# A decoder layer on one core: the QKV projection of three token tiles in three f32r passes, with the front's banks and the loads rearranged

## The reference

```python
x = x + attn(layernorm(x), Wq, Wk, Wv, Wo)        # 32 query heads, 8 key/value heads of 16
x = x + xattn(layernorm(x), ctx, Wq2, bq, Wk2, bk)  # context 2 x 512 x 512
x = x + ffn(layernorm(x), w_gate, w_up, w_down)     # ternary weights, inner size 1376

def attn(x, Wq, Wk, Wv, Wo):
    q, k, v = x @ Wq, x @ Wk, x @ Wv                # 512, 128 and 128 columns
    q, k = rope(q), rope(k)
    scores = q @ k.T / 4, causal mask, softmax      # per head
    return (attn @ v) @ Wo
```

## Time and profile before

| what | value |
|---|---|
| device time, median of 3 runs | 246.92 us (246.51 to 247.06) |
| the profiled execution's own time | 245.21 us |
| its span in the profile | 243.5 us |
| PE busy | 230.0 us, 94% |
| DVE busy | 153.6 us, 63% |
| ACT busy | 119.5 us, 49% |
| POOL busy | 36.1 us, 15% |

### The profile page before, as it was taken

How to read it: one execution, slowest core, us unless ns; L and a number is a source line. 1 busy time by engine, 2 the same in 40 slices (tenths; PEclk the granted TensorE clock), 3 DMA queues, 4 the chain that set the end, 5 groups by cost and what they waited for, 6 DMA issues and landing times.

```text
span 243.5 us, 4183 instructions
## 1 busy us (share of the span) xinstructions
PE 230.0 (94%) x1454; PEld 160.6 (66%) x1454; DVE 153.6 (63%) x561; ACT 119.5 (49%) x199; POOL 36.1 (15%) x61
## 2 busy tenths in 40 slices
PE   8799999999998979999999998899999999999994
PEld 3367657677766757655776454688888777767771
DVE  2689389996775687687571358986645655343323
ACT  2036576666849636662597370843643223323230
POOL 3330000372222224221220221000000010000000
PEclk9999999999999997999999999999999999999999
DMA  5999200001650460346000054000000000020002
GB/s 155 393 401 405 87 0 1 1 3 48 241 182 1 119 232 0 91 133 245 3 2 2 0 191 156 1 3 0 0 1 3 0 0 3 0 89 0 0 3 86
DMA packets 8981, 19.97 MB, mean 82 GB/s; under 512 B 1056, under 2 KB 1440, under 8 KB 8960
## 3 DMA queue, kind: packets, MB, share of 16 engines
q1 hardware_dynamic: 8384, 19.60, 22.7%
q10 hardware_dynamic: 576, 0.10, 0.2%
HBM read 18.58 MB, written 1.05 MB: 81 GB/s over the span
## 4 chain that ended last, share of the span: by engine, by line
PE 81%; DVE 7%; DMA 5%; issue 2%; ACT 2%; POOL 1%; DVEq 0%; SPq 0%; ACTq 0%; POOLq 0%
PE ps L1193 16%; PE ps L1208 8%; PE ps L1032 7%; PE ps L1058 7%; PE ps L1131 6%; PE ps L1084 6%; PE ps L1019 4%; PE ps L1040 4%; PE ps L1286 3%; PE ps L1300 3%; PE ps L1146 3%; PE ps L1115 3%; PE ps L1257 3%; DMA raw<-up_dram 2%; PE ps L1250 2%
## 5 line engine op out<-in xcount | busy, mean ns | idle before, releaser
L912 DVE CUSTOM_DVE_ANT_0 ps<-ps,maskf 128x128 f32<-128x128 f32 (+1 forms) x128 | 41.1, 397 | 3.0 <-PE ps L1250 3.0
L492 POOL TENSOR_SCALAR_AFFINE_SELECT prob<-prob 128x512 f32<-128x512 f32 x32 | 20.1, 651 | 94.1 <-ACT prob L688 94.1
L688 ACT ACTIVATE prob<-ps 128x1536 f32<-128x1536 f32 x16 | 23.2, 1451 | 16.4 <-PE ps L1289 16.4
L1032 PE MATMUL ps<-wqkv,xnT 128*128 128x512 f32 (+1 forms) x64 | 22.3, 493 | 0.7 <-ACT xnT L509 0.7
L576 ACT CAST in_hi<-inter 128x256 f16<-128x256 f32 (+1 forms) x22 | 8.9, 406 | 24.0 <-DVE inter L874 24.0
L1193 PE MATMUL ps<-h_hi,gate_q 128*128 128x256 f16 (+1 forms) x88 | 20.4, 273 | 0.0
L1193 PE MATMUL ps<-h_lo,up_q 128*128 128x256 f16 (+1 forms) x88 | 20.4, 273 | 0.0
L1193 PE MATMUL ps<-h_lo,gate_q 128*128 128x256 f16 (+1 forms) x88 | 20.4, 273 | 0.0
L1193 PE MATMUL ps<-h_hi,up_q 128*128 128x256 f16 (+1 forms) x88 | 20.4, 272 | 0.0
L874 DVE TENSOR_TENSOR inter<-gate_s,ps 128x256 f32<-128x256 f32 (+1 forms) x22 | 9.2, 420 | 16.4 <-PE ps L1193 15.4
L912 DVE DVE_READ_ACCUMULATOR2_ANT mx<- 128x1 f32 x128 | 18.5, 145 | 0.0
(11 more groups left out here) (161 smaller groups left out, 468.4 us busy)
## 6 DMA issues: line engine op xcount, KB each, us to landing
raw<-gate_dram SPq DMA_DIRECT2D x1, 2752.0 KB, 17.2
raw<-up_dram SPq DMA_DIRECT2D x4, 688.0 KB, 4.9
ctxT<-ctxT_dram SPq DMA_DIRECT2D x2, 1024.0 KB, 5.9
ctx_n<-ctx_dram SPq DMA_DIRECT2D x2, 1024.0 KB, 8.7
wqkv<-wqkv_dram SPq DMA_DIRECT2D x4, 384.0 KB, 6.3
raw<-down_dram SPq DMA_DIRECT2D x2, 768.0 KB, 4.6
x<-x_dram SPq DMA_DIRECT2D x4, 256.0 KB, 5.8
xwq<-xwq_dram SPq DMA_DIRECT2D x1, 1024.0 KB, 9.1
```

Source lines behind the costliest of these rows:

```text
L492: nc.gpsimd.affine_select(out=v, in_=v, compare_op=ALU.is_ge, fill=0.0, base=0, pattern=[[0, GROUP], [1, P]], channel_multiplier=-1).then_ ...
L688: nc.scalar.activation(prob[:, i % 2, :], ps[:, 3:6, :].rearrange("p a b -> p (a b)"), ACT.Exp, scale=DH ** -0.5).then_inc(exp_done, 1)
L912: nc.vector.tensor_tensor_reduce(scores, scores, mask, 1.0, LOWEST, ALU.add, ALU.max, to).then_inc(max_done, 1)
L1032: mm = nc.tensor.matmul(out, xnT[:, k, t * P:(t + 1) * P], wqkv[:, k, lo:hi], start=(k == 0), stop=(k == KD - 1))
```

## The change

The projections of tiles 1, 2 and 3 are computed as three products of f32r operands in place of one of f32. Tile 0 stays as it was. For this the weights are split once, in four chunks of 128 x 640: ACT rounds each to f32r (`w_hi`), POOL subtracts to get the rest (`w_lo`). The transposed tile is split too: ACT's copy out of PSUM now rounds (`xnT_r`), and DVE subtracts that from the bank (`tile_low`, `xnT_lo`). DVE no longer copies two of the ten early stacks, ACT copies them all. The projections and stacks use other banks. Side pieces stand in other slots, and the loads of the up weights, of the context of batch 0 and of the down weights are spread over more steps; every up chunk has a semaphore of its own.

```diff
-        TILE_BANK = (0, 5, 6, 7)
+        TILE_BANK = (0, 5, 6, 0)
+        ST_BANKS = (5, 1, 6, 2)
...
-            ([], [("abs", 0, 1), ("abs", 0, 2)], [("pq", 3)]),
-            ([("abs", 0, 3)], [("rot", 3, 0)], [("pk", 3), ("st", 10), ("hi", 3, 0)]),
-            ([("hi", 3, 1), ("rot", 3, 1)], [("a", 0, 0), ("part", 0)], [("st", 11)]),
+            ([("abs", 0, 1)], [("abs", 0, 2)], [("pq", 3)]),
+            ([], [("rot", 3, 0), ("abs", 0, 3), ("pk", 3)], [("rot", 3, 1), ("part", 0), ("a", 0, 0)]),
+            ([], [("lo", 3, 0), ("st", 10), ("hi", 3, 0)], [("st", 11), ("hi", 3, 1)]),
...
-            ([("abs", 1, 0)], [], [("abs", 1, 1), ("a", 2, 0)]),
-            ([], [], [("abs", 1, 2), ("u", 0)]),
-            ([("abs", 1, 3)], [("part", 1)], [("u", 1)]),
+            ([], [("abs", 1, 0)], [("abs", 1, 1), ("a", 2, 0)]),
+            ([], [("abs", 1, 2)], [("u", 0)]),
+            ([], [("part", 1), ("abs", 1, 3)], [("u", 1)]),
...
-        UP_LOADS, CTX_LOAD, DOWN_LOADS = {4: (0, 1), 5: (2, 3)}, 8, {11: (0, 1), 12: (2, 3)}
+        UP_LOADS, CTX_LOAD, DOWN_LOADS = {4: (0,), 5: (1,), 6: (2,), 7: (3,)}, 8, {11: (0,), 12: (1,), 13: (2, 3)}
...
-                    load_context(0)
+                if CTX_LOAD <= i < CTX_LOAD + KD:
+                    k = i - CTX_LOAD
+                    sp.dma_start(ctxT[0][:, k, :], ctxT_d[0, k * P:(k + 1) * P, :]).then_inc(ctxT_in[0], 16)
+                if CTX_LOAD + KD <= i < CTX_LOAD + KD + PT:
+                    k = i - CTX_LOAD - KD
+                    sp.dma_start(ctx_n[0][:, k, :], ctx_d[0, k * P:(k + 1) * P, :]).then_inc(ctx_in[0], 16)
...
-            for n in range(1, TT):
-                root(n)
+            def w_low(k):
+                pool.wait_ge(w_high, k + 1)
+                nc.gpsimd.tensor_tensor(w_lo[:, k, :], wqkv[:, k, :], w_hi[:, k, :].bitcast(F32), ALU.subtract
+                                        ).then_inc(w_low_done, 1)
+
+            root(1)
+            w_low(0)
+            root(2)
+            w_low(1)
+            root(3)
+            w_low(2)
+            w_low(3)
...
             tile_T(0)
+            for k in range(KD):
+                act.wait_ge(wqkv_in[k], 16)
+                nc.scalar.copy(w_hi[:, k, :], wqkv[:, k, :]).then_inc(w_high, 1)
             tile_T(1)
             heads_high(0, 0)
             heads_high(0, 1)
             tile_T(2)
             tile_T(3)
-            stacks(0, 1)
+            stacks(0, 5)
             heads_high(1, 0)
             heads_high(1, 1)
-            stacks(1, 2 * NST)
+            stacks(5, 2 * NST)
...
+            def tile_low(t):
+                dve.wait_ge(xnT_sb, t + 1)
+                nc.vector.tensor_tensor(xnT_lo[:, :, (t - 1) * P:t * P],
+                                        bank(TILE_BANK[t]).rearrange("p (k q) -> p k q", k=KD),
+                                        xnT_r[:, :, t * P:(t + 1) * P].bitcast(F32), ALU.subtract
+                                        ).then_inc(xnT_low, 1)
...
                 stats(t)
+                if t == 3:
+                    tile_low(1)
                 normalise(t, lambda: t >= 2 and dve.wait_ge(xnT_ps, t - 1))
...
                 rotate(t, 1)
                 if t == 1:
-                    stacks()
+                    tile_low(3)
                 heads_low(t, 0)
                 heads_low(t, 1)
+                if t == 0:
+                    tile_low(2)
...
+            def project_high(out, t, e):
+                pe.wait_ge(xnT_sb, t + 1)
+                pe.wait_ge(w_high, KD)
+                pe.wait_ge(xnT_low, t)
+                for k in range(KD):
+                    nc.tensor.matmul(out, xnT_r[:, k, t * P:(t + 1) * P], w_hi[:, k, HEAD_COLS[e]],
+                                     start=(k == 0), stop=False)
+                    nc.tensor.matmul(out, xnT_lo[:, k, (t - 1) * P:t * P], w_hi[:, k, HEAD_COLS[e]],
+                                     start=False, stop=False)
+            def project_low(out, t, e):
+                for k in range(KD):
+                    pe.wait_ge(w_low_done, k + 1)
+                    mm = nc.tensor.matmul(out, xnT_r[:, k, t * P:(t + 1) * P], w_lo[:, k, HEAD_COLS[e]],
+                                          start=False, stop=(k == KD - 1))
...
             tile_T(0)
+            pe.wait_ge(xnT_sb, 1)
+            project_first(qkv_bank(0, 0), 0).then_inc(qkv_ps, 1)
+            tile_T(1)
+            project_first(qkv_bank(0, 1)[:, 0:QKV - D], 1).then_inc(qkv_ps, 1)
+            project_high(qkv_bank(1, 0), 1, 0)
+            tile_T(2)
+            project_high(qkv_bank(1, 1)[:, 0:QKV - D], 1, 1)
+            project_low(qkv_bank(1, 0), 1, 0).then_inc(qkv_ps, 1)
+            project_low(qkv_bank(1, 1)[:, 0:QKV - D], 1, 1).then_inc(qkv_ps, 1)
             tile_T(3)
             stacks(0)
+            project(qkv_bank(2, 0), 2, 0).then_inc(qkv_ps, 1)
+            stacks(1)
             pe.wait_ge(rope_read, 4)
             pe.wait_ge(v_sb, 2)
-            pe.wait_ge(xnT_sb, 3)
-            project(qkv_bank(2)[:, 0:D], 2, 0).then_inc(qkv_ps, 1)
-            stacks(1)
-            project(qkv_bank(2)[:, D:QKV], 2, 1).then_inc(qkv_ps, 1)
+            project(qkv_bank(2, 1)[:, 0:QKV - D], 2, 1).then_inc(qkv_ps, 1)
```

More of the change, by code:

```diff
@@ L68, in decoder_layer @@
         gate_q = sb("gate_q", [P, KD, INNER], BF16)
+        front = ExitStack()
+        sb("front_places", [P, QK], F32, front)
+        xnT_lo = sb("xnT_lo", [P, KD, 3 * P], F32R, front)
+        front.close()
         up_q = sb("up_q", [P, KD, INNER], BF16)
@@ L125, in decoder_layer @@
         ksT = sb("ksT", [P, KV // 2, B * T], F32R, early)
+        front = ExitStack()
+        w_lo = sb("w_lo", [P, KD, QKV], F32R, front)
+        front.close()
         prob = sb("prob", [P, 2, 6 * T], F32, early)
         early.close()
+        w_hi = qsT[1][:, :, :].rearrange("p a b -> p (a b)")[:, 4 * T:4 * T + KD * QKV].rearrange("p (k n) -> p k n", k=KD)
         late = ExitStack()
@@ L162, in decoder_layer @@
         m_placed = [sem("m_placed0"), sem("m_placed1")]
+        up_in = [sem(f"up_in{k}") for k in range(KD)]
         out_stored = sem("out_stored")
@@ new lines, in decoder_layer @@
+            ([("whole", 1, 3), ("tern", 1, 1), ("tern", 1, 2)], [("tern", 1, 3), ("wo", 1)], [("n2", 0), ("n2", 1),
+             ("a", 3, 0), ("xT", 1, 0)]),
+            ([], [("xT", 1, 1)], [("a", 3, 1), ("high", "wo", 0), ("low", "wo", 0)]),
+            ([("abs", 2, 0), ("abs", 2, 1), ("g", 0, 0), ("abs", 2, 2)], [("high", "wo", 1), ("abs", 2, 3)],
+             [("low", "wo", 1), ("g", 0, 1), ("high", "wo", 2)]),
+            ([("low", "wo", 2), ("xs", 0), ("part", 2)], [("abs", 2, 4)], [("xs", 1), ("xpT", 0), ("high", "wo", 3)]),
@@ L508, in tile_T @@
                 act.wait_ge(xnT_ps, t + 1)
-                nc.scalar.copy(xnT[:, :, t * P:(t + 1) * P],
+                nc.scalar.copy((xnT if t == 0 else xnT_r)[:, :, t * P:(t + 1) * P],
                                bank(TILE_BANK[t]).rearrange("p (k q) -> p k q", k=KD)).then_inc(xnT_sb, 1)
@@ L531, in stacks @@
                 for s in range(lo, hi):
[L532 to L535 removed]
+                    act.wait_ge(stT_ps, s + 1)
+                    nc.scalar.copy(st_target(s), bank(st_bank(s)).rearrange("p (a q) -> p a q", a=4)
+                                   ).then_inc(stT_act, 1)
             def sum_abs(w, c):
                 rows, at, n = chunks(w)[c]
[L540 to L543 removed]
+                if w == 1:
+                    act.wait_ge(up_in[c], 16)
+                elif c == 0:
+                    act.wait_ge(raw_in, 16 * (1 if w == 0 else 2 + KD))
+                if w == 1 and c == 0:
+                    act.wait_ge(rope_read, 2 * TT)
                 nc.scalar.activation(tern_target(w)[0:rows, at:at + n], raw[0:rows, at:at + n], ACT.Abs,
@@ L1317, in _ @@
             pe.wait_ge(consts_set, 3)
-            for s in range(2 * NST - 3, 2 * NST):
+            for s in range(2 * NST - len(ST_BANKS), 2 * NST):
                 st_evacuated(pe, s)
```

119 lines of the change are left out of this document (52 added, 67 removed), and 7 rows, old and new, of the table BESIDE.

## The result

The changed kernel takes 249.41 us, the median of 4 runs (249.25 to 249.57); the kernel before takes 246.71 in 4 runs (244.84 to 247.06). The ratio is 1.0116, 95% interval 1.0068 to 1.0165: about 1.2% slower, where 243.1, faster, was forecast. The profiled execution took 249.52 us with a span of 247.8, against 245.21 and 243.5 before: 4.3 us to explain.

The account below looks back on a forecast made before the run. PE's work plus its few holes bounds the kernel, DVE nearly full at 36.4 to 49.5 us. Front +0.1, tile 3 +0.2, up -1.35, context -2.8: -3.85 from 246.92 gives 243.1 us, range 240.8 to 246.2.

Parts of the forecast that it names:

- the one on the down loads: Later steps: the last down chunks leave one step later, close to the sums that read them; no cost counted.
- new holes between 100 and 156 us, where I count none: Sign that the prediction is wrong: PE gets new idle times in that stretch, where it expected none.
- The front: Up to group 0: POOL's 1.4 us subtractions hold three DVE normalisations; PE waits 1.75 against 1.66 gained, 0.1 us lost.
- The prediction's own rate: Front's end: with normalisations held three times, each 0.1 us more of POOL's subtraction costs 0.3 us.
- held twice: Rival, front: last normalisation waits for POOL's third and fourth subtractions; 244.5 us, or 246.0 with a clock fall; chance 0.2.
- no hold: Rival, front: POOL's subtraction leaves DVE alone, or takes 0.75 us; PE saves 1.66 without waits; 241.3 us, chance 0.19.
- Tile 3: Early steps where DVE is full: PE's 0.83 us saving costed at nothing; 0.2 lost, between 1.0 lost and 0.5 gained.
- The load terms: Steps 8 and 11: spread up loads gain 1.35 us; spread context loads, with the clock there, gain 2.8.
- The f32r prices: Projection products on PE: f32r passes at 0.23 us a step for 512 columns and 0.13 for 256.
- The rows from step 7 on: Later steps, with AFTER's reordering: no change of time counted; AFTER changes no amount of work, PE is full there.

Follow-up runs that it names:

- e1: after with the last three down chunks issued at i = 12, in place of one at 12 and two at 13; 244.20 us, ratio 0.9883 to the kernel before.
- e4: The kernel before with only the down loads moved as in the change, one step later; 247.01 us, ratio 1.0013 to the kernel before.
- e5: after with late down loads kept and, in step 15, gT's evacuation ahead of the second sum in ACT's order; 247.30 us, ratio 1.0009 to the kernel before.
- e7: e1 with POOL waiting for the normalisations of tiles 1, 2 and 3 before its first three subtractions; 241.94 us, ratio 0.982 to the kernel before.
- after: The changed kernel, with the whole change, against the kernel before; 249.41 us, ratio 1.0116.
- e11: e8 with the three POOL waits of e7; 240.34 us, ratio 0.9782 to the kernel before.
- e8: after's front, f32r products and separate semaphores, with BESIDE, AFTER, UP_LOADS and DOWN_LOADS of the kernel before; 242.37 us, ratio 0.9857 to the kernel before.
- e10: e9 with the three POOL waits of e7; 238.94 us, ratio 0.9719 to the kernel before.
- e3: The kernel before with only the context spread over eight DMAs and a semaphore for each up chunk; 240.35 us, ratio 0.9772 to the kernel before.
- e12: e3 with after's table rows from step 7 on and its AFTER; 239.65 us, ratio 0.9768 to the kernel before.
- e9: e1 with the kernel before's table rows for steps 0 to 6; 239.81 us, ratio 0.977 to the kernel before.

## Why the prediction was wrong

**The step that failed** is the one on the down loads: "the last down chunks leave one step later than before, close to the sums that read them", costed at nothing. Measured: +5.9 us in the profile, 5.2 by e1's median. The lateness was seen and its price was not worked out. What was to be added: the load leaves at 117.66 behind a context chunk and needs 7.6 us to the sum that reads it, the new row of step 15 puts two sums of 1.25 us ahead of `gT`, and PE waits for `gT`: 3.06 us, and 2.82 more by the clock behind it. e4 shows that the late load alone is free, e5 that the second sum, with the fall of the clock, is 3.3 us of it in the profile and 2.1 in the median. The warning "new holes between 100 and 156 us, where I count none" is what happened.

**The front**: the mechanism was right, the size off. The prediction had POOL start just before the normalisation and hold it for the whole subtraction, three times; all three rows show it, and e7 shows the cost. But it took 1.4 us for the subtraction, for 640 columns; it is 1.82 for 768. Normalisations of 1.6 were forecast and 2.03 found; the rotation of tile 0, forecast for 17.5, began at 19.12, and the front's last projection at 32.8 in place of 30.7. The prediction's own rate, 0.3 us for each 0.1 of the subtraction, gives 0.1 + 3 x 0.42 = 1.4 us; e1, whose front has no fall of the clock, lost just that (27.57 against 26.14 before). After's other 0.8 of the +2.2 are the late start of tile 1's normalisation, 0.4, which is none of the change's doing as far as the rows show, and 0.4 that wasn't counted: half the clock from about 18 to 22 us, behind PE's hole of 2.30 (the rival "held twice" had such a fall in it). e5, which has the same fall, has the same front, 27.97 us. The figure of the Trainium skill (GPSIMD Engine Reference, 3.1 Elementwise — side-by-side cycle accounting), scaled to 768 columns, is an estimate of 1.7 us, near the 1.82 measured. The rival "no hold" had it that PE then saves its 1.66 us and waits for nothing. With POOL's waits nothing is held, and 0.3 to 0.5 us arrive: PE waits for `w_lo` instead, 1.24 us in e7 and 0.58 in e11, a wait that neither the forecast nor a rival has.

**Tile 3**: "0.2 lost, between a loss of 1.0 and a gain of 0.5". The product did get shorter, and PE only waited longer for the maxima (0.81 to 0.83 us in e1, e7 and e8, in place of 0.18), as argued. e8 puts the f32r part at nothing: 14.82 us for groups 0 to 3, before 14.87. The new rows cost some 1.2 us without the clock and 2.5 to 3.0 with it, by e7 and e10, outside the bounds. The clock was missed: the argument counted PE's holes there by their length only.

**The load terms** were right: -1.7 and -3.1 in the profile against -1.35 and -2.8. There is no hole for `oT` in step 8 or for the placed maxima in step 11, and the clock is 1.00 from 88 to 98 us. The nearness has some luck in it: the forecast was made from one profiled execution, and e3 makes them 6.5 us in the median, since falls of the clock behind these two holes go too, and the profiled execution had one of them only.

**The f32r prices** were right: 0.23 us a pass of 512 columns and 0.12 of 256 (0.13 forecast). **The rows from step 7 on** and `AFTER`, costed at nothing, gain 0.5 to 0.7 us (e12). Of the rivals, "held twice" had the front's fall of the clock, but not its mechanism: the last normalisation ended at 19.20, with POOL's third subtraction, and not at 20.9 with the fourth. None had the down load.

From after's 249.41 the way down is: 5.2 for the down load (e1), 2.3 for the three holds (e7), 3.0 for the rows of steps 0 to 6 (e10); by the ratios, which allow for the chips, 5.7, 1.6 and 2.5. What is left, 8 us below before, is for the most part spread loads (6.5, e3) and later rows (0.7, e12); the f32r passes have half a us of it at most.

What stays open: why the clock falls at 45 to 50 us in some executions of a kernel and not in others, why after's down load took 1.3 us longer than e4's, and why e9's first subtraction came late.

## What to carry to other kernels

A load that is moved "close to its reader" is to be costed as a chain: when it leaves its queue and behind what, how long it takes, what the reading engine has queued between the landing and the next thing that PE needs. Work given to POOL isn't free because POOL is idle: a subtraction that starts first holds a tensor-scalar or a two-input add of DVE to its end, and a wait that lets DVE's short instruction go first cost POOL 0.66 us each time, and three of them gave 2.3 in the median. The bill comes later: the last subtraction ends later, and PE waits for it. Shorter products pay only where PE's own work sets the end: with the operand split on slower engines, tile 1 ended later than in plain f32, and of 1.66 us saved 0.3 to 0.5 arrived.

## What the runs showed of the hardware

- A hole on PE may be followed by 3.4 or 6.8 us at half the clock, and the hole's length didn't settle it: in the same place of step 8 the clock stayed whole behind 1.35 us (the kernel before) and fell behind 1.08 (e4). Behind 3.06 us it fell (after), behind 1.54 it did not (e5); right behind holes of 0.68 and 0.28 us it fell in e1 and e7. In e8 a fall from about 8 to 14 us cost nothing: the execution that had it took 242.3, one at full clock 242.2. PE reached tile 1 at 17.27 with no wait there; `xnT_lo` was ready at 17.12, and in after PE had idled 2.30 us for it.
- The accumulator form of DVE's tensor-scalar took 0.81 us beside POOL's subtraction, where the plain form, 0.55 alone, took 2.03; the two-input add took 2.05 beside POOL and 0.69 alone.
- A tenth of a us decides who is held. In e8 the subtraction's row starts 0.08 us after the normalisation's, and the normalisation still took 2.18; in e9 it starts 0.17 us after, and the normalisation took 0.55. Counted from that normalisation, e9's front was 1.0 to 1.1 us shorter than those of e1 and e8.
